# Four attention layers on one core: the weighted sum with the turned probabilities as the stationary operand and a column of ones beside the values

## What is computed

```python
h = jnp.maximum(_layernorm(x), 0.0); x = x + L0(h, adj)   # dot product, one head
h = jnp.maximum(_layernorm(x), 0.0); x = x + L1(h, adj)   # dot product, 4 heads, leaky relu, mean over heads
h = jnp.maximum(_layernorm(x), 0.0); x = x + L2(h, adj)   # additive scores sum_f a_f * leaky(u_if + v_jf), elu
h = jnp.maximum(_layernorm(x), 0.0); x = x + L3(h, adj)   # leaky(src_i + dst_j), residual, elu, layer norm
# in each layer, per graph and head:
attention = softmax(where(adj > 0, scores, -large), axis=-1)   # 1024 x 1024
out = attention @ values                                       # values: 1024 x 64
```

## Time and profile before

| | us |
|---|---|
| median of three runs | 3885.69 (3883.1 to 3893.41) |
| profiled execution | 3882.72 |
| span of its instructions | 3880.8 |
| L0, units | 31 to 310 |
| L1, units | 362 to 1385 |
| L2, units | 1461 to 3485 |
| L3, units | 3515 to 3866 |

### The profile page before, as it was taken

One profiled execution on the slowest core, in us unless ns is written; L12 is line 12 of the kernel. 1 busy time (PEld: TensorE's weight loads), 2 busy tenths in 40 slices (PEclk: granted clock), 3 DMA queues, 4 the chain that ended last, 5 costly groups with the idle time before them and its releaser, 6 DMA issues. The chain is left out here.

```text
span 3880.8 us, 81004 instructions
## 1 busy us (share of the span) xinstructions
PE 3269.0 (84%) x31339; PEld 1730.1 (45%) x31339; DVE 3276.1 (84%) x6456; ACT 3046.8 (79%) x3649; POOL 992.1 (26%) x565
## 2 busy tenths in 40 slices
PE   7997999999999968888788887887887878878776
PEld 5664666666666633233232232332322322226665
DVE  7776887888888778999999899899999998975776
ACT  3444777777777769899899998998999989975665
POOL 4333555555555600000000000000000000005664
PEclk9998999999999989999999999999999999998887
DMA  6550000000000000000000000000000000001111
GB/s 188 176 172 21 18 18 18 18 18 18 18 18 18 17 10 9 8 11 10 9 9 7 9 12 7 9 12 7 11 8 9 11 8 9 12 4 50 52 52 44
DMA packets 65885, 110.39 MB, mean 28 GB/s; under 512 B 24563, under 2 KB 24564, under 8 KB 65524
## 3 DMA queue, kind: packets, MB, share of 16 engines
q1 hardware_dynamic: 65524, 105.44, 9.0%
HBM read 86.55 MB, written 18.87 MB: 27 GB/s over the span
## 5 line engine op out<-in xcount | busy, mean ns | idle before, releaser
L919 ACT ACTIVATE l_scalar_ring<-l_w,l_r 128x1024 f32<-128x1024 f32 x1728 | 1812.9, 1143 | 33.1 <-DVE l_values L965 25.8
L1018 DVE TENSOR_SCALAR l_vector_ring<-l_w_code,l_r_code 128x1024 f32<-128x1024 f32 x2368 | 1621.6, 758 | 3.3 <-issue 0.4
L849 PE MATMUL scores<-l_scalar_ring,l_signs 128*32 128x512 f32 x6912 | 849.5, 610 | 91.5 <-ACT l_scalar_ring L919 91.4
L859 PE MATMUL scores<-l_vector_ring,l_signs_code 128*32 128x512 f16 x9472 | 657.1, 399 | 260.6 <-DVE l_vector_ring L1018 255.3
L226 ACT COPY probs_t<-turned 128x512 f32<-128x512 f32 x512 | 293.0, 586 | 508.3 <-PE turned L196 505.1
L407 POOL TENSOR_TENSOR l_masked<-l_relu,mask 128x1024 f32<-128x1024 f32 x256 | 545.7, 2132 | 489.1 <-ACT l_relu L531 456.2
L207 PE MATMUL outT<-probs_t,l_values 128*64 128x128 f32 x7168 | 514.5, 284 | 48.5 <-ACT probs_t L226 28.5
L859 PEld LDWEIGHTS scores<-l_vector_ring,l_signs_code 128*32 128x32 bf16 x9472 | 222.2, 96 | 735.5 <-DVE l_vector_ring L1018 496.3
L207 PEld LDWEIGHTS outT<-probs_t,l_values 128*64 128x64 f32 x7168 | 404.0, 140 | 283.4 <-DVE l_acc L615 110.3
L196 PE MATMUL turned<-ident,l_probs 128*128 128x128 f32 x3072 | 433.7, 286 | 11.1 <-issue 7.0
L849 PEld LDWEIGHTS scores<-l_scalar_ring,l_signs 128*32 128x32 f32 x6912 | 206.7, 111 | 493.4 <-issue 292.6
(11 more groups left out here) (207 smaller groups left out, 3284.8 us busy)
## 6 DMA issues: line engine op xcount, KB each, us to landing
mask<-masks_kept SPq DMA_DIRECT2D x192, 256.0 KB, 2.6
l_adj<-adj SPq DMA_DIRECT2D x64, 512.0 KB, 4.2
masks_kept<-mask SPq DMA_DIRECT2D x64, 256.0 KB, 2.3
x_res<-x SPq DMA_DIRECT2D x8, 256.0 KB, 5.0
out<-x_res SPq DMA_DIRECT2D x8, 256.0 KB, 3.4
l_wqk<-L_gnn_Wq SPq DMA_DIRECT2D x2, 64.0 KB
l_wqk<-L_gnn_Wk SPq DMA_DIRECT2D x2, 64.0 KB
l_wv<-L_gnn_Wv SPq DMA_DIRECT2D x1, 64.0 KB
```

Of the source, the lines that this page charges most:

```text
L849: last = nc.tensor.matmul(s.scores[g * ROWS:(g + 1) * ROWS, buf, half, :], signs[:, window], scalar_ring[:, at % SCALAR_RING, g, halves[ha ...
L859: last = nc.tensor.matmul(s.scores[g * ROWS:(g + 1) * ROWS, buf, half, :], signs_code[:, par, window], parts(vector_ring[:, at % VECTOR_RI ...
L919: last = nc.scalar.activation(scalar_ring[:, at % SCALAR_RING, g, :], w[:, par, :], ACT.Relu, bias=r[:, par, column:column + 1])
L1018: last = nc.vector.tensor_scalar(vector_ring[:, at % VECTOR_RING, g, :], w_code[:, par, :], r_code[:, par, column:column + 1], None, ALU.max)
```

## The change

In all four layers the operands of `probs_times_values` change places: `probs_t` is stationary (128x128) and `values` moving, with a 65th column of ones beside the 64 values, so that the result comes out with rows on partitions and the row sum in column 64. `turn_out`, `copy_out`, `add_halves`, `turned_out`, `rowsum` and `accum_out` of the exponential are gone. `finish` waits for `out_ready`, takes the reciprocal of the 65th column and scales from PSUM. In L0 and L1 VectorE does `finish(u-1)` ahead of `copy_half(u)`. In L2 `finish` moves from set 1 of the run after next to set 15 of the same run in which the product is made. The rings, the fills and the scores stay as they are.

```diff
-def probs_times_values(pe, s, sems, values, u):
+def probs_times_values(pe, s, sems, values, u, out, buffers=1):
     pe.wait_ge(sems["half0_copied"], STARTS + u + 1)
     pe.wait_ge(sems["half1_copied"], STARTS + u + 1)
-    wait(pe, sems["out_copied"], STARTS + u)
+    wait(pe, sems["unit_done"], STARTS + u + 1 - buffers)
     for j in range(s.NB):
-        half = j % 2
-        last = s.nc.tensor.matmul(s.outT[half * s.D:(half + 1) * s.D, 0:P], values[:, j, :], s.probs_t[:, j, :],
-                                  start=(j < 2), stop=(j >= s.NB - 2))
+        last = s.nc.tensor.matmul(out[:, 0:s.D + 1], s.probs_t[:, j, :], values[:, j, :], start=(j == 0),
+                                  stop=(j == s.NB - 1), skip_group_check=True)
     last.then_inc(sems["out_ready"], 1)
...
-def turn_out(pe, s, sems, u, fills_done, to=None, buffers=1):
-    pe.wait_ge(sems["out_copied"], STARTS + u + 1)
-    if to is None:
-        wait(pe, sems["fill_copied"], fills_done)
-    wait(pe, sems["unit_done"], STARTS + u + 1 - buffers)
-    s.nc.tensor.matmul((s.fill if to is None else to)[:, 0:s.D], s.turned_out[:], s.add_halves[:], start=True,
-                       stop=True).then_inc(sems["out_turned"], 1)
...
-def copy_out(v, s, sems, u):
-    v.wait_ge(sems["out_ready"], u + 1)
-    s.nc.vector.tensor_copy(s.turned_out[:], s.outT[:, 0:P]).then_inc(sems["out_copied"], 1)
...
-    s.nc.scalar.activation(probs, logits, ACT.Exp, bias=s.negmax[:, slot:slot + 1], scale=scale,
-                           accum_out=s.rowsum[:, slot:slot + 1]).then_inc(sems["probs_ready"], 1)
+    s.nc.scalar.activation(probs, logits, ACT.Exp, bias=s.negmax[:, slot:slot + 1], scale=scale
+                           ).then_inc(sems["probs_ready"], 1)
...  L0 and L1
-        values = sb("values", [P, 2, NB, H, D], F32)
+        values = sb("values", [P, 2, NB, H, D + 1], F32)
...
                     turn_probs(pe, s, sems, probs[:, n % 2, :], u)
-                    if n > 0:
-                        turn_out(pe, s, sems, u - 1, 0, unit_out)
...
-                turn_out(pe, s, sems, b * U + U - 1, 0, unit_out)
...
-                nc.vector.reciprocal(s.rinv[:, slot:slot + 1], s.rowsum[:, slot:slot + 1])
-                v.drain()
-                v.wait_ge(sems["out_turned"], u + 1)
+                v.wait_ge(sems["out_ready"], u + 1)
+                nc.vector.reciprocal(s.rinv[:, slot:slot + 1], unit[:, D:D + 1])
+                v.drain()
...
-                    copy_half(v, nc.vector.tensor_copy, s, sems, 0, u)
                     if n > 0:
                         finish(b, n - 1, u - 1)
+                    copy_half(v, nc.vector.tensor_copy, s, sems, 0, u)
...
-                    copy_out(v, s, sems, u)
...
+            for par in range(2):
+                for j in range(NB):
+                    nc.vector.memset(values[:, par, j, :, D:D + 1], 1.0)
...  L2
-        MAX, EXP, TURN, COPY, MULTIPLY, COPY_OUT = 3, 6, 7, 10, 11, 14
-        TURN_OUT, FINISH = 0, 1
+        MAX, EXP, TURN, COPY, MULTIPLY, FINISH = 3, 6, 7, 10, 11, 15
...
-                    if k == TURN_OUT and u > 1:
-                        turn_out(pe, s, sems, u - 2, issued)
...
-                    if k == COPY_OUT:
-                        copy_out(v, s, sems, u - 1)
+                    if k == FINISH:
+                        finish((n - 1) % NB, 1 - buf, u - 1)
...  L3
-                    if not (first and n == 0):
-                        turn_out(pe, s, sems, u - 1, 0, unit_out[(n - 1) % 2], buffers=2)
...
-                    copy_out(v, s, sems, u)
```

More of the change, by code:

```diff
@@ L583, in take_fill @@
                     at = (k - 2 - PIECES * QK) * each
-                    last = nc.vector.tensor_copy(values[:, par, at:at + each, :, :].rearrange("p j h d -> p (j h d)"), bank[:])
+                    last = nc.vector.tensor_copy(values[:, par, at:at + each, :, 0:D],
+                                                 bank[:].rearrange("p (j h d) -> p j h d", j=each, h=H))
                 last.then_inc(sems["fill_copied"], 1)
@@ L661, in _ @@
             for p in range(2):
-                nc.vector.tensor_reduce(bound[:, p:p + 1], s.outT[:, p * H * D:(p + 1) * H * D], AX.X, ALU.max)
+                nc.vector.tensor_reduce(bound[:, p:p + 1], s.out[:, p * H * D:(p + 1) * H * D], AX.X, ALU.max)
             v.drain()
@@ L756, in additive_layer @@
         scores = [s.scores[:, i, :, :].rearrange("p a b -> p (a b)") for i in range(2)]
+        unit_out = s.out[:, 0:D + 1]
         block = ctx.enter_context(nc.Block())
@@ L820, in _, with fill @@
         def _(pe):
-            def fill(b, par, k, units):
+            def fill(b, par, k):
                 bank = fill_bank(s, b, k)
                 wait_for_bank(pe, s, sems, b, K, k, 0 if k < 2 else 4 if 4 <= k < 8 else 2)
-                wait(pe, sems["unit_done"], STARTS + units)
                 both = [slice(h * BANK, (h + 1) * BANK) for h in range(2)]
@@ L862, in sum_set, with run @@
                     last.then_inc(sems["vector_summed"], 1)
-            def run(b, par, n, u, buf, fills, issued, before=True):
+            def run(b, par, n, u, buf, fills, before=True):
                 first, count = fills
@@ L886, in run @@
                     if k == MULTIPLY:
[L887 to L888 removed]
+                        probs_times_values(pe, s, sems, values[:, prev, :, :], u - 1, unit_out)
             def graph(b, par):
[L891 removed]
                 for n in range(NB):
                     project = b + 1 < B
[L894 removed]
+                    run(b, par, n, b * NB + n, n % 2, fills_of(n, project), before=(b > 0 or n > 0))
             pe.wait_ge(sems["weights_ready"], 2)
@@ L901, in _ @@
             for k in range(K):
-                fill(0, 0, k, 0)
+                fill(0, 0, k)
             for b in range(B):
@@ L905, in _ @@
             last = B * NB - 1
-            turn_out(pe, s, sems, last - 1, B * K)
             turn_probs(pe, s, sems, logits, last)
-            probs_times_values(pe, s, sems, values[:, 1, :, :], last)
-            turn_out(pe, s, sems, last, B * K)
+            probs_times_values(pe, s, sems, values[:, 1, :, :], last, unit_out)
         @block.scalar
@@ L1045, in run @@
                         code_signs(1 - par)
-                    if k == FINISH and u > 1:
-                        finish((n - 2) % NB, buf, u - 2)
-                        if n == 1:
-                            batch_end(b - 1)
+                    if k == BATCH and n == 1 and b > 0:
+                        batch_end(b - 1)
                     if not before:
@@ L1172, in gat_layer @@
         total = sb("total", [P, 8, NB], F32)
-        unit_out = [s.scores[:, 1, i, :] for i in range(2)]
+        unit_out = [s.scores[:, 1, i, 0:D + 1] for i in range(2)]
         block = ctx.enter_context(nc.Block())
@@ L1289, in fill, with graph @@
                 last.then_inc(sems["fill_ready"], 1)
-            def graph(b, par, project, first=False):
+            def graph(b, par, project):
                 for n in range(NB):
@@ L1306, in _ @@
                 fill(0, 0, k)
-            graph(0, 0, True, first=True)
+            graph(0, 0, True)
             with pe.Fori(0, (B - 4) // 2) as t:
@@ L1313, in _ @@
             graph(B - 1, 1, False)
-            turn_out(pe, s, sems, B * NB - 1, 0, unit_out[1], buffers=2)
         @block.scalar
@@ L1441, in graph @@
                         logit((n + 2) % NB, u + 2)
-                    for k in fills[:1]:
-                        take_fill(b + 1, 1 - par, k)
-                    copy_out(v, s, sems, u)
-                    for k in fills[1:]:
+                    for k in fills:
                         take_fill(b + 1, 1 - par, k)
@@ L1511, in _ @@
             nc.vector.memset(s.ident[:], 0.0).then_inc(zeroed, 1)
-            v.wait_ge(ones_ready, 2)
-            nc.vector.tensor_tensor(s.add_halves[:], s.ident[:, 0:s.D], s.ident[:, s.D:2 * s.D], ALU.add)
         @block.gpsimd
```

58 lines of the change are left out of this document (26 added, 32 removed).

## The result

The changed kernel took 3936.14 us in the median of four runs (3930.08 to 3947.3), the kernel before beside it 3889.55 (3883.1 to 3897.38): a ratio of 1.0122 with a 95% interval of 1.0091 to 1.0153. The forecast was 3913 us, slower, range 3850 to 3970. The profiled execution of after is its slowest run, 3947.3 us with a span of 3945.2, at a mean granted clock of 0.955; the other three have 0.960 to 0.963.

A forecast was written before the change was run, and what follows sets the result against it. TensorE was taken as the path in L1 and mostly L0, VectorE as pacing L2, no engine full in L3. L0 +19, L1 +81, L2 -100, L3 +28 gave +28 us on 3882.7; predicted 3913 us, range 3850 to 3970.

The forecast's parts named there:

- two waits that go away in L2: L2: VectorE's waits per unit, 1.55 us for `turn_out` and 0.56 us for the product, would go.
- The product, 1.82 us: All layers: 16 matmuls take 1.82 us, 0.79 more than before, loads setting the rate; 1.70 below, 1.98 above.
- Fill units of L1, 4.56 us: L1, 154 units with a fill: TensorE's transposes, scores, fill and product add up to 4.56 us, 702 us in all.
- Unfilled units, 3.70 us: L1 units without a fill: the loop between TensorE and VectorE takes 3.70 us, with `finish` covered by the transposes.
- In a unit with a fill it is hidden by TensorE's scores and fill: L1: the leaky part of `finish`, 0.93 us more on VectorE, lies beside TensorE's 1.81 us of scores and fill.
- 4.24 us for an unfilled unit: L1, unfilled unit after each fourth unit: the leaky part makes the copy about 0.54 us late, 4.24 us.
- L2, -100 us: L2: VectorE loses `copy_out` and two waits, so the layer is 100 us shorter, bounds 60 to 147.
- rival of 60 us: L2 stalls on a new pace of ScalarE or TensorE and gives only 60 us: 3954 us, chance 20%.
- that of 147: L2 pays back everything, VectorE and ScalarE both full, 147 us gained: 3867 us, chance 30%, faster.
- L0, +19 us: L0, 64 units: a mean of 0.3 us more for each, +19 us, bounds 0 to 40.
- L3, +28: L3: 0.43 us more for each of 64 units, +28 us, bounds +5 to +50.
- The clock was a rival: L3: a third of 64 products at the lower clock level cost 0.79 us more each, +17 us; no separate chance.

The follow-up runs named there:

- one-column run: Changed kernel with the product's moving operand cut from 65 columns to the column of ones, weighted sums left out: 4239.81 us.
- the 128 columns: Changed kernel with the moving operand of L3's product padded from 65 to 128 columns with ones: 3903.52 us, 1.0045 of before.

## Why the prediction was right, and where its steps were off

The outcome was right by its main sum: a longer product on TensorE where TensorE is the path, against two waits that go away in L2. Two steps inside it were off by some 50 and 35 us with opposite signs, and a third by 21. That the sum came out on the right side owes something to luck: with the fill units at the 4.33 us they took and all else as forecast, it would have been 3878 us, no clear change. The 35 us too many there stood in for most of what the leaky part cost.

**The product, 1.82 us: right.** 1.73 behind a fill and 1.84 without one. The one-column run shows that loads set the rate.

**Fill units of L1, 4.56 us: 0.23 too long.** The step is 4.33. I took start-to-start times of the old order for transposes and fill (0.93 and 0.95, they are 0.88 and 0.86) and 1.82 for the product. 154 x 0.23 = 35 us too many.

**Unfilled units, 3.70 us: right**, 3.66. `finish` is indeed covered by the transposes where it has no leaky part.

**"In a unit with a fill it is hidden by TensorE's scores and fill": this step failed.** I priced the leaky part at 0.93 us from the earlier trace rows, a case in which line 619 takes 0.39 us. It was held up there too, but not for long: it started late in GpSimd's addition, which ended at 598.16, and ended itself at 598.24. In the new order `finish` follows the product at once, which puts line 597 under GpSimd's mask addition in 62 of 64 cases, and the copy behind it becomes late: a fill unit with a leaky part takes 5.17 us. Where I put it on the path, 4.24 us for an unfilled unit, it is 5.23. Taking the leaky part off the path gives 66.6 us; the sum had 25 unfilled units with 0.54 us, 14 us. That is 53 us too few. Together with the fill units' 35 too many it makes most of L1's 23.

The page "SBUF — State Buffer" of the Trainium skill (SBUF: two separate sides) has a rule for this: a VectorE instruction with two SBUF inputs and a GpSimd instruction that reads SBUF exclude each other, and the one that comes second is blocked until the first is done. The trace agrees: line 597 ends 0.08 us after GpSimd's, and takes 0.23 us once it has one SBUF input. The prediction did not ask which instructions the new order puts side by side.

**L2, -100 us: -79.** The mechanism is as forecast: VectorE's waits at the two steps are all but gone. The size was a guess between 60 and 147. A unit took 32.0 us before (2016.0 over the 63 steps from the first transposes to the last) and 30.75 after, where I had 30.5. VectorE's waits in the earlier trace rows were 2.1 us a unit; after, the rows shown add up to 55 us for 56 units, 0.98 each. Of the 2 us that went, nearly 0.9 came back as waits for transposes and fills (48.6 us in the window, 5.5 in that of before), which the sum had at nothing. VectorE and ScalarE rose together from 92% to 96%. The rival of 60 us was nearer in size than that of 147, but neither engine became the sole bound.

**What the gain of L2 is due to.** The prediction named the place of `finish` as the gain's source, and that holds for the old form: 49 us for one set, 67.6 with `copy_out`'s set. It isn't the only remedy, since the new form in the old place gains the same 79 us.

**L0, +19 us: +11.2**, within its bounds of 0 to 40. I didn't look into it further. **L3, +28: +22.9.** The 22.9 is from one execution; between the means of four kernels each it is 16. The clock has as much to say as the product: with it at 0.98 the same form is 28 us faster than before, not 23 slower. The clock was a rival in the prediction, with +17 us; it should have been asked what the clock costs in the kernel before as well, where it is 0.84. An L3 of the old form at the full clock and with its short product was not run, so how much of the 28 us the clock gives and how much the form stays open. At 0.78 of the full clock, 44% of 370 us or 163 us ran at the lower level, and 51 came back with the 128 columns.

## What to carry to other kernels

Price a moved instruction in its new company and not by its old duration: look which instruction of the other engine will run beside it, and keep what the next copy doesn't need behind that copy. Before a new form is written to remove a wait, move the waiting step by one slot: here one step gave 49 of 78 us, two gave 67.6. Where narrow matmuls with 128-column loads fill a stage and its granted clock is low, as in L3 here, try wider moving operands: it costs one run to know.

## What the runs showed of the hardware that I had not expected

- Kernels that differ only in the moving columns of the product differ in granted clock. L1: 0.98 with 65 columns and 0.83 with one, with TensorE busy for 1249 of 1290 us. L3: 0.78 with 65 columns and 0.98 with 128, and the layer some 50 us shorter. And with the same columns, L3 of the old form had 0.84 with its matmuls side by side and 0.97 with one behind the other. The runs show the connection, not why.
- A VectorE instruction of 64 elements a partition took 1.32 us in place of 0.23, because it has two SBUF inputs and started while GpSimd added two SBUF tensors; it ended 0.08 us after that. With one input in PSUM it took 0.23 us beside the same addition.
- At the full clock, 128 moving columns cost 1.84 us a product (L3), against 1.73 to 1.84 with 65 and 1.71 with one (L1).
